# One PSUM bank for all small products and three for the maxima, in a two-layer gated cross-attention and expert kernel

## What is computed

```python
q, k, v = split_heads(query @ Wq + bq), split_heads(key @ Wk + bk), split_heads(value @ Wv + bv)
weights = softmax(einsum('bhqd,bhkd->bhqk', q, k) / sqrt(8))          # layer 1: masked where mask == 0
out = einsum('bhqk,bhkd->bhqd', weights, v).reshape(b, -1, 128) @ Wo + bo
x = x + tanh(g_xattn) * out
gates = top 2 of 8 of softmax (layer 1: sigmoid) of layernorm(x) @ gate_w, normalised
h = gelu(einsum('td,edf->etf', xf, w1) + b1)
y = einsum('etf,efd->etd', h, w2) + b2
x = x + tanh(g_ffn) * (sum over the two chosen experts of gate * y)
```

## Time and profile before

| | before |
|---|---|
| median of 3 executions | 1013.98 us (1012.92 to 1014.5) |
| the profiled execution: time, span in the trace | 1013.23 us, 1011.4 us |
| TensorE busy (matmuls) | 899.4 us, 89% |
| VectorE, ScalarE, GpSimd busy | 730.1, 588.1, 516.9 us |
| granted TensorE clock, mean | 0.972 of full |

### The profile page before, as it was taken

One profiled execution on the slowest core, in us unless ns is written; L12 is line 12 of the kernel. 1 busy time (PEld: TensorE's weight loads), 2 busy tenths in 40 slices (PEclk: granted clock), 3 DMA queues, 4 the chain that ended last, 5 costly groups with the idle time before them and its releaser, 6 DMA issues.

```text
span 1011.4 us, 32583 instructions
## 1 busy us (share of the span) xinstructions
PE 899.4 (89%) x13088; PEld 651.2 (64%) x13088; DVE 730.1 (72%) x1576; ACT 588.1 (58%) x1077; POOL 516.9 (51%) x662
## 2 busy tenths in 40 slices
PE   3888998989899898988999999999999899999975
PEld 1355676766767676776767776666666666666754
DVE  5675876868678587786867858777787778787723
ACT  2155666575755757557475575757666575757560
POOL 5544554545445354553555456676666576662211
PEclk9978999999999999999999999999999999999995
DMA  6245432212222122222656656676766656675200
GB/s 158 77 123 150 129 112 92 80 49 73 70 84 78 51 68 72 80 79 67 119 116 127 138 96 142 137 156 127 156 148 121 140 124 143 137 137 99 55 2 19
DMA packets 103554, 104.47 MB, mean 103 GB/s; under 512 B 28442, under 2 KB 97388, under 8 KB 103404
## 3 DMA queue, kind: packets, MB, share of 16 engines
q1 hardware_dynamic: 101986, 102.07, 43.3%
q10 hardware_dynamic: 1418, 0.32, 0.2%
HBM read 35.89 MB, written 0.46 MB: 36 GB/s over the span
## 4 chain that ended last, share of the span: by engine, by line
PE 58%; DVE 25%; ACT 9%; issue 6%; DMA 1%; ACTq 1%; SPq 0%; DVEq 0%
DVE mx L1072 14%; PE pO L1208 13%; PE pMX L1229 10%; PE pST L1187 8%; PE pKV L1274 6%; PE pKV L1265 6%; PE pFH L1399 5%; PE pFY L1328 3%; ACT P L789 2%; DVE rden L1014 2%; ACT HR L798 2%; DVE HR L970 2%; ACT L789 2%; PE pFY L1332 2%; DVE ysc L1043 1%
## 5 line engine op out<-in xcount | busy, mean ns | idle before, releaser
L1072 DVE TENSOR_REDUCE mx<-pMX 112x1 f32<-112x500 f32 x768 | 487.4, 668 | 127.9 <-PE pMX L1229 125.0
L789 ACT ACTIVATE P<-pST 125x448 f32<-125x448 f32 x768 | 389.6, 542 | 277.7 <-PE pST L1187 272.4
L1229 PE MATMUL pMX<-kop,qmax 48*112 48x500 f16 (+1 forms) x768 | 284.3, 408 | 50.1 <-DVE mx L1072 37.3
L1187 PE MATMUL pST<-qexp,kop 50*128 50x112 f16 (+2 forms) x3072 | 266.7, 215 | 13.0 <-ACT P L789 7.9
L1187 PEld LDWEIGHTS pST<-qexp,kop 50*128 50x128 f16 (+2 forms) x3072 | 183.7, 100 | 78.0 <-issue 23.8
L1208 PE MATMUL pO<-P,V 125*17 125x112 f32 x6144 | 188.5, 264 | 0.0
L1229 PEld LDWEIGHTS pMX<-kop,qmax 48*112 48x112 f16 (+1 forms) x768 | 97.4, 129 | 124.0 <-DVE mx L1072 57.6
L1208 PEld LDWEIGHTS pO<-P,V 125*17 125x17 f32 x6144 | 138.1, 98 | 35.0 <-issue 18.7
L641 POOL CAST khi<-kfull 128x500 f16<-128x500 f32 x96 | 57.7, 601 | 190.1 <-ACT kfull L816 188.6
L643 POOL TENSOR_TENSOR klo<-kfull,khi 128x500 f16<-128x500 f32 x96 | 108.8, 1134 | 7.8
L732 POOL TENSOR_TENSOR Clo<-C,Chi 128x500 f16<-128x500 f32 x93 | 105.7, 1137 | 7.5
(11 more groups left out here) (151 smaller groups left out, 1106.8 us busy)
## 6 DMA issues: line engine op xcount, KB each, us to landing
C<-in_ctxT SPq DMA_DIRECT2D x31, 750.0 KB, 6.7
kop<-maskop SPq DMA_DIRECT2D x48, 437.5 KB
kop<-khi SPq DMA_DIRECT2D x192, 62.5 KB
kop<-khi SPq DMA_DIRECT2D x96, 125.0 KB
kop<-klo SPq DMA_DIRECT2D x96, 62.5 KB
kop<-klo SPq DMA_DIRECT2D x48, 125.0 KB
maskin<-in_mask SPq DMA_DIRECT2D x8, 656.2 KB, 5.5
qexp<-qmax SPq DMA_DIRECT2D x16, 182.0 KB
```

What stands on the lines that cost most here:

```text
L789: nc.scalar.activation(P[0:KP, slot, h * 4 * T:(h + 1) * 4 * T], pST[0:KP, h, 0:4 * T], ACT.Exp, scale=EXP_SCALE).then_inc(exp_done, 1)
L1072: nc.vector.tensor_reduce(mx[:, s % 2, c, p:p + 1], pMX[0:T, m % 2, 0:CW], AX.X, ALU.max).then_inc(max_done, 1)
L1187: mm = nc.tensor.matmul(pST[0:keys.stop - keys.start, h, i * T:(i + 1) * T], kop[rows, b, slot, keys], qexp[rows, b, slot, :, :].rearrange ...
L1229: nc.tensor.matmul(pMX[0:T, m % 2, 0:CW], qmax[rows, b, slot, :, :].rearrange("r j q -> r (j q)"), kop[rows, b, slot, c * CW:(c + 1) * CW] ...
```

## The change

- PSUM: pFH and pFY become one bank pF with one list of uses, `f_uses`; the bank set free is a third one for pMX. Maximum m may be issued when maximum m-3 has been reduced.
- Places: "ct" moves from the end of slot 0 into the middle of slot 1, "h0" into the middle of slot 10 (from its end), "sum" of even steps from the end of slot 5 into the middle of slot 6, "yb" from 4 to 3, "gT" from 7 to 6, "h6" and "h7" from 4 and 5 to 7 and 8. `is_mid` names those that are issued between the first maximum and the second of the slot and read out between them too.
- Layer 0's first expert product: instead of one float32 matmul for each of 4 chunks, three f16 matmuls (high by high, high weight by low activation, low weight by high activation). The weights are split once, in steps 2 and 3, on ScalarE (high) and GpSimd (low); the activations at "xT", by two more VectorE instructions.
- Denominators: `V` has a second column of ones, `headmask` becomes two columns, and `OM` holds 112 columns in place of 224. "sum" is 112 columns wide, `rden` too, GpSimd's two instructions too, "y" needs two matmuls in place of four. `OM` now takes two VectorE instructions, and moves ahead of the reading out of small products in slot 5.
- The residual addition of odd steps leaves VectorE for GpSimd, which does it in two instructions (scale, add); the last one stays.

```diff
-VW = PR + 1
+VW = PR + 2
...
+def f_uses(s):
+    ct = [(1, "ct", 1)] * has_m(s - 1)
...
     if has_end(s) and not sums_last(s):
-        uses += [(1, "y2", 0), (2, "y3", 1), (4, "yb", 1)]
+        uses += [(1, "y2", 0), (2, "y3", 1), (3, "yb", 1)]
     if is_batch(s - 2):
-        uses.append((5, "sum", 1))
+        uses.append((6 - s % 2, "sum", 1))
...
+        uses += [(9, "xT", 1), (10, "h0", 1), (10, "lg", 1), (11, "h1", 1)]
     if has_f(s):
-        uses.append((7, "gT", 1))
+        if layer0:
+            uses += [(k, f"h{e}", 1) for e, k in zip(range(2, 8), (0, 1, 2, 3, 7, 8))]
+        uses.append((6, "gT", 1))
...
+def is_mid(s, use):
+    return use in ("ct", "h0") or use == "sum" and s % 2 == 0
...
-        pMX = ps("pMX", [128, 2, 512])
+        pMX = ps("pMX", [128, 3, 512])
...
-        pFH = ps("pFH", [128, 512])
-        pFY = ps("pFY", [128, 512])
+        pF = ps("pF", [128, 512])
...
                 if has_end(s) and not ends(s):
...
+                    link(nc.gpsimd.tensor_scalar(acc[:, 1, :], acc[:, 1, :], gains[0:T, g:g + 1], None, ALU.mult))
...
+                    nc.gpsimd.tensor_tensor(xg((s - 5) // 2), acc[:, 1, :], acc[:, 0, :], ALU.add).then_inc(x_done, 1)
...
+                    if s in (2, 3) and kt in (1, 3, 5, 7):
...
+                        nc.scalar.activation(w1hi[:, e, :], w1raw[:, raw_columns(e)], ACT.Copy).then_inc(w1_hi, 1)
...
-                        nc.vector.reciprocal(rden[:, :], pFY[:, 0:2 * T]).then_inc(fy_free, 1)
+                        nc.vector.reciprocal(rden[:, :], pF[:, 0:T]).then_inc(f_free, 1)
...
                     elif use == "xT":
...
+                            link(nc.vector.tensor_copy(xnfT[:, :], pF[:, 0:T]))
+                            link(nc.vector.tensor_copy(xfhi[:, :], pF[:, 0:T]))
+                            nc.vector.tensor_tensor(xflo[:, :], pF[:, 0:T], xfhi[:, :], ALU.subtract).then_inc(f_free, 1)
...
                     if kt == AV_LAG and is_batch(s - 2):
...
+                        link(nc.vector.tensor_scalar(om, of[:, 0], headmask[:, 0:1], None, ALU.mult))
+                        nc.vector.scalar_tensor_tensor(out=om, in0=of[:, 1], scalar=headmask[:, 1:2], in1=om,
+                                                       op0=ALU.mult, op1=ALU.add).then_inc(o_free, 1)
+                    for back, use in issued_before(f_uses, s, kt):
+                        from_f(back, use)
...
                         largest(m)
+                    for use in [u[1] for u in f_uses(s) if u[0] == kt and is_mid(s, u[1])]:
+                        from_f(0, use)
...
-                if n > 0 or m > 1:
-                    pe.wait_ge(max_done, NMAX * n + m - 1)
+                if n > 0 or m > 2:
+                    pe.wait_ge(max_done, NMAX * n + m - 2)
...
+                        if l == 0:
+                            for c in range(F0C):
+                                for i, (w1, x_) in enumerate(((w1hi, xfhi), (w1hi, xflo), (w1lo, xfhi))):
+                                    mm = nc.tensor.matmul(pF[:, c * T:(c + 1) * T], w1[:, e, c * 128:(c + 1) * 128],
+                                                          x_[:, :], start=(i == 0), stop=(i == 2))
...
                         for h in range(2):
                             max_scores(st, m0 + h)
                             score_half(st, kt, h)
+                            if h == 0:
+                                mids(kt)
```

More of the change, by code:

```diff
@@ L982, in from_fh @@
+                            w("b1_1").unsqueeze(2).broadcast_to([128, 4, T]), ALU.add).then_inc(f_free, 1)
+                    else:
+                        nc.vector.tensor_scalar(HR[0:F1, 4, :], pF[0:F1, 0:T], bs1b[:, 0:1], None, ALU.add
+                                                ).then_inc(f_free, 1)
                 def from_fh(back, use):
                     if use == "qT":
-                        ready(fh_ready, fh_uses, back, use)
-                        nc.vector.tensor_copy(xnqT[:, :], pFH[:, 0:T]).then_inc(fh_free, 1)
@@ L986, in from_fh @@
-                        nc.vector.tensor_copy(keepT[:, :], pFH[0:1, 128:128 + T]).then_inc(fh_free, 1)
+                        ready(f_ready, f_uses, back, use)
+                        nc.vector.tensor_copy(xnqT[:, :], pF[:, 0:T]).then_inc(f_free, 1)
+                        nc.vector.tensor_copy(keepT[:, :], pF[0:1, 128:128 + T]).then_inc(f_free, 1)
                     elif use == "q":
-                        ready(fh_ready, fh_uses, back, use)
+                        ready(f_ready, f_uses, back, use)
@@ L1004, in from_fy @@
                 def from_fy(back, use):
-                    ready(fy_ready, fy_uses, back, use)
+                    ready(f_ready, f_uses, back, use)
                     l = layer_of(s - back - 2)
@@ L1077, in step @@
                 for kt in range(KT):
+                    if s == 3 and kt == 11:
+                        dve.wait_ge(w1_split, E0)
                     if s == 1 and kt == 8:
@@ L1228, in max_scores @@
                     rows, slot = slice(0, SHIFT0), i
-                nc.tensor.matmul(pMX[0:T, m % 2, 0:CW], qmax[rows, b, slot, :, :].rearrange("r j q -> r (j q)"),
+                nc.tensor.matmul(pMX[0:T, m % 3, 0:CW], qmax[rows, b, slot, :, :].rearrange("r j q -> r (j q)"),
                                  kop[rows, b, slot, c * CW:(c + 1) * CW], start=True, stop=True).then_inc(mx_ready, 1)
@@ L1336, in step, with issue, mids @@
+                def issue(use):
+                    if use in ("qT", "q") or use[0] == "h":
+                        product(use)
+                    else:
+                        small(use)
+                def mids(kt):
+                    for use in [u[1] for u in f_uses(s) if u[0] == kt and is_mid(s, u[1])]:
+                        issue(use)
                 for kt in range(KT):
@@ L1341, in step @@
                     late = kt in (1, 7)
-                    experts = [u[1] for u in fy_uses(s) if u[0] == kt and early(u[1])]
+                    experts = [u[1] for u in f_uses(s) if u[0] == kt and early(u[1])]
                     if experts:
@@ L1411, in _ @@
+                    for use in [u[1] for u in f_uses(s) if u[0] == kt and not is_mid(s, u[1]) and not early(u[1])]:
+                        issue(use)
             run_steps(step)
```

300 lines of the change are left out of this document (151 added, 149 removed).

## The result

The changed kernel takes 986.71 us (984.43 to 990.22, 4 executions), the one before 1013.45 beside it: ratio 0.975, interval 0.973 to 0.977, 26.7 us less. 958 was forecast, so the direction held and half of the gain came. The profiled execution is the slowest of the four: 990.22 us, 23 us less than the profiled one before; its span is 988.1 us, its clock 0.954 of full (0.972 before).

The account below looks back on a forecast made before the run. TensorE (busy 89%) was taken as the bound, with VectorE's maxima between its pieces. Layer 0 (14.4 and 15.4 us), layer 1 (14.4 and 7), drain 3 and start 1 made 55 us off 1013.2: 958, range 928 to 987.

Parts of the forecast that it names:

- TensorE's work: On TensorE, h products save 15.4 us (0.73 us each, 0.68 to 0.78), sum 7.2, y 7.4: together 30 us less.
- the rival that rested on this: Layer 0's f16 expert products win nothing: their 15 us go, time 973; chance 8%.
- VectorE's work: On VectorE, net 25 us less to do (rden, residual, against OM and split), worth something only where TensorE waits for it.
- The third bank: In pMX, TensorE runs one maximum further ahead, so 0.6 us more of VectorE's lateness is hidden until the next heavy slot.
- careful-walk rival: Waits for maxima vanish almost wholly, 55 of 77 us, and the 30 us of work come through: 928; chance 12%.
- Even steps of layer 0: Steps 4 to 18, even: 1.8 us won in each of 8, 14.4 us; from slot 9 on nothing.
- The walk: TensorE and VectorE followed through a step of layer 0 at the trace's prices: even reaches slot 9 at 20.7, odd takes 27.9.
- Odd steps of layer 0: 27.9 us for 30.1, so 2.2 us won in each of 7, 15.4 us.
- Layer 1: Steps 19 to 31: even ones win 2.4 us each, 14.4 in all, odd ones 1.0 each, 7 in all.
- The single bank: Small products share one bank, 288 handovers, mostly a slot apart; ct waits for h2's read, a new hole of 0.65 us.
- dear-bank rival: Half of the small bank's 288 handovers cost 0.2 us more than walked: 29 us go, 987; chance 10%.
- The ct transfer: Rival: ct's rows reach slot 3's scores 0.8 us late in each of 28 steps: 22 us go, 980; chance 10%.

Follow-up runs that it names:

- full_denominators: The changed kernel with the old denominators again (one ones column, sum and rden over 224 columns, OM in one instruction, y in four matmuls): 994.41 us, 0.9812.
- two_small_banks: The changed kernel with two banks for the small products, used in turn, and two for the maxima: 1000.43 us, 0.9894.
- residual_on_dve: The changed kernel with the residual addition of the group's end back on VectorE, in one instruction: 990.08 us, 0.9765.
- gelu_l1: The changed kernel with ScalarE's GELUs ahead of slot 9's exponentials in layer 1 alone: 982.76 us, 0.9708.
- gelu_both: The changed kernel with h6 in slot 4, h7 in slot 7, and ScalarE's GELUs ahead of slot 9's exponentials in both layers: 993.79 us, 0.98.

## Where the prediction was right and where it failed

- **TensorE's work: right.** 0.69 us for the h product lies in its bounds; undoing the parts costs 1.7 and 0.85 us a pair of layer 0 where the prediction's terms are 1.9 and 0.9. The Trainium skill, TensorE: Matmul & The Clock Gate, section Back-to-back issue gap, gives 81 ns a matmul of 128 columns in such a stream; by it, as an estimate, the product would have taken 0.97 us. The trace shows 0.05 us from start to start at 112 columns, and the rival that rested on this fell.
- **VectorE's work: sized right, worth nothing.** rden measures 0.84 us (0.77 forecast), the OM pair 0.70 with its link (0.6 forecast). The prediction itself said that this counts only where TensorE waits for VectorE; full_denominators shows no more than TensorE's share.
- **The third bank: the direction right, the size wrong; the step that failed is the netting.** "0.6 us more lateness hidden" let the waits for maxima fall under 25 us (17.1), and undoing it costs 34 us. But the forecast booked freed waits as time won: 1.2 us in a pair of layer 0 (4.0 less 2.8 of work), 2.5 in one of layer 1 (3.4 less 0.9). Of the 3.0 and 1.8 us that came, undoing the work's terms accounts for 2.55 and 0.67, which leaves 0.45 and 1.15 for waits; by TensorE's idle time it is -0.4 and 0.1 (busy time is modelled, and counts some waiting as work). By the larger ones, 8 pairs and 6 are 14 of the 19 us missing in steps 4 to 31. The careful-walk rival's condition, that the waits for maxima vanish, came nearly true, and its 928 us did not: TensorE, let ahead of VectorE's maxima, met the next thing that was late.
- **A reading under it was too high.** The 57.6 us of the earlier trace rows are waits of weight loads. Its matmuls stood idle ahead of maxima for less, in the same view of the kernel before:

```profile
PE pMX L1229 <- DVE mx L1072: 37.3, 98, 1.5
```

With 11.0 for OM and 4.9 for HR that is 53 us of holes, not 77.

- **Even steps of layer 0: right.** The walk has slot 9 at 20.7 us; its first maximum starts at 20.87 (22.54 before), and the step won 1.75 for 1.8. In it 1.01 us of waits for maxima went and waits for ScalarE grew by 1.14, 0.69 of them at y0, whose wait the walk left at 0.36: what was late next (table load, GELUs, table load, six exponentials) was seen and not priced. The halved sum and six cheaper products are what paid.
- **Odd steps of layer 0: wrong, 0.93 us a step, 6.5 us in all.** The walk took off "some 2.5 us of waits for maxima and cc"; TensorE's whole idle time there was 2.33, of it 1.75 ahead of maxima. And the single bank took more than was booked: y behind q 0.86 and h0 behind xT's reads 0.64 were in the walk (0.5 and 1), y2 behind ct's copy 0.39 was called "as before" where no such hole was, and yb waits 0.24. None of this is ScalarE's, and removing the table loads left these steps at 28.40.
- **Layer 1: wrong by most.** Even steps won 1.4 for 2.4 and odd ones 0.46 for 1.0, 10 us in all. In the even ones the maxima's 1.09 went, and waits for ScalarE grew by 0.58, and the weighing of slot 6 now waits 0.65 us until OM's two instructions have read pO (0.34 with one, in full_denominators). In the odd ones 0.98 went, and y behind q (0.48), the sum (0.37) and y2 behind ct (0.19) came.
- **The single bank: mechanism right, in part undersized.** ct waits for HR 0.59 (0.65 forecast). Whole, two_small_banks shows 20 us, 6 of them in the drain. The measured time is the dear-bank rival's 987, but that is a coincidence as far as the runs tell: the rival wanted 29 us beyond the walk, and the walk had most of these holes in it.
- **The start and the drain: wrong.** In the profiled execution step 2's hole grew from 3.2 us to 5.8, and TensorE's clock was half for 20.5 us around it (6.8 before). One profile doesn't size this: the hole is 3.8 to 4.8 us in the six other kernels with the same start (residual_on_dve, the three other places of the h products, gelu_l1 and gelu_both), and their step 4 begins at 121 to 126 us (125.5 in the changed kernel). It is 3.3 to 3.5 in the three kernels with two banks of maxima, where TensorE comes to it later. Of the drain's 3 us none came: turning h0 and lg gave nothing, and a second small bank gives 6 (above), so there it is y0 to y3 on one bank.
- **The ct transfer**, the 980 us rival, fell: behind step 2 the scores wait for it once, 1.1 us in the drain. **The clock** was in no term; see below.

## What to carry to other kernels

Price a freed wait by what the engine meets next, partner by partner and step by step: here the buffer that let TensorE run ahead of VectorE's maxima brought it earlier to ScalarE's block of 6.6 us in even steps, and to the reads that empty the one small bank in odd ones, and its idle time stayed. Take the wait from the engine's own idle time, not from its weight loads'. An order that moves a wait and leaves the pair of steps the same to 0.03 us was a sign here that another engine's total between two points holds it. And compare periods by a mark that the change doesn't move, or over a whole cycle of the pipeline.
